# The first batch's transition matrix in units of four target tiles by two source tiles, and its first propagation over four chunks at once in eight PSUM banks

## The chip, the cores and the metric

The kernel runs on one core of one Trainium2 chip. The metric is the device time of one execution in microseconds. Three runs of the kernel before gave 760.93, 761.02 and 761.81 us; their median, 761.02 us, is the time that a forecast is made against. A time below, such as 60.26, is counted in microseconds from the start of the span in the profiled execution.

## The reference, cut to what matters

```python
def _L0_gnn_ref(X, A, Wv, bv, aw, ab, Wk, bk):      # X = relu(layernorm(x)), B = 8, N = 1024, D = 256
    Xw = X @ Wv + bv
    sj, si = Xw @ aw[:d, 0], Xw @ aw[d:, 0]
    e = leaky_relu(sj[:, None, :] + si[:, :, None] + ab[0], negative_slope=0.2)
    alpha_matrix = A * exp(e)
    transition = alpha_matrix / (sum(alpha_matrix, axis=-1, keepdims=True) + 1e-12)
    H, Xk = 0, X
    for k in range(3):
        H = H + Xk @ Wk[k] + bk[k]
        Xk = einsum('bij,bjd->bid', transition, Xk)
    return relu(H)

def _L1_gnn_ref(X, A, kernel, bias):
    Ah = A + eye(N)
    dh = rsqrt(sum(Ah, axis=-1))
    return relu(einsum('bnm,bmf,fc->bnc', dh[:, :, None] * Ah * dh[:, None, :], X, kernel) + bias)

x = x + _L0_gnn_ref(relu(layernorm(x)), adj, ...)
x = x + _L1_gnn_ref(relu(layernorm(x)), adj, ...)
```

## The kernel before, in words

N = 1024 rows are eight tiles of 128. Each fp32 operand of a large product is split into a rounded part (`_hi`, an fp32r copy made by ACT) and a remainder (`_lo`, a subtraction by DVE or POOL), and a product is three matmuls: hi by hi, hi by lo, lo by hi.

`T` is the unnormalised transition matrix, transposed, and is held whole in SBUF as `t_hi` and `t_lo`. It is made in eight units of 1024 columns. In the kernel before, a unit is two target tiles by four source tiles. For each unit ACT forms the leaky scores (`leaky`, line 533, four instructions of 256 columns) and their exponential (`exponent`, 539), DVE multiplies by the adjacency (`t_prod`, 822), ACT rounds (`t_high`, 547), and DVE forms the remainder (`t_low`, 827). Unit `u` needs the adjacency block that the SP or ACT queue has loaded into `tg_a`.

A batch goes through five stages on PE. **U** is the first propagation, eight chunks (one per target tile) of 24 matmuls each. DVE takes each finished chunk out of its bank (`u_chunk`, lines 841, 843, 848, into `tmp`), ACT rounds it (589) and POOL forms its remainder (404). **Dense** is `layer0_dense` of the next batch: for each of its eight tiles six matmuls of 512 columns into `da` and six of 258 into `db`. **V** is the second propagation, **Z** the propagation of layer 1, and the output product follows. In the first batch the units of T are still being made while U runs, so `accumulate_halves` (line 1207) takes chunks 2 to 7 in halves, one half per unit.

The order of all engines is written out by hand: dictionaries name, for each step of a stage, which side work an engine does there (lines 41 to 46, and `rounding` at 584 and `centring` at 911). The side work that matters here, in the first batch's U stage:

- `rows(b, t)` on ACT (564) sums row tile `t` of the adjacency from one of four slots `a_raw`. When it ends, the SP queue loads tile `t + 4` into the slot (276), or, for the last four, the first chunks for Z (290). `diag` (873) on DVE needs the first of those chunks.
- The mean of the next batch is turned by PE into `mean_bank`, a part of `tp` (1084), copied by ACT (`mean_copy`, 452), stored and loaded back as a broadcast by SP (308, 312).
- `centre` (759, DVE) subtracts that mean from the next batch's input, a group of two tiles at a time, `centred_hi` (460, ACT) rounds the group and `centred_lo` (765, DVE) forms its remainder. Dense cannot begin before group 0 is ready.
- Dense of batch 1 also waits until DVE has emptied the banks that U used (`g1_tmp_ready` at 1138), and each tile of `db` waits until DVE has taken the tile before (`dense0`, 780 and 782).

## Time and profile before

| | |
|---|---|
| median of 3 runs (lowest, highest) | 761.02 us (760.93, 761.81) |
| the profiled execution's own time | 761.23 us |
| its span | 759.4 us |
| PE (matmuls), busy in the span | 744.8 us (98%) |
| PE weight load | 684.5 us (90%) |
| DVE | 623.9 us (82%) |
| ACT | 535.4 us (71%) |
| POOL | 188.3 us (25%) |
| mean DMA rate | 189 GB/s |
| U stage of batch 0, first matmul to last matmul's start | 34.27 to 58.20 us |
| dense stage of batch 1, first matmul | 60.26 us |
| V stage of batch 0, first matmul | 79.98 us |

The table is read from the bottom up. PE is busy nearly all the time, so what a change is worth is read from the short stretches in which PE stands still; those in question lie between 34 and 80 us. Busy times are averages over stages that have different limits and don't say which engine the others wait for there. In a row of a timeline, the first number is the start and the second the busy time. Instructions of one engine overlap a little, so the step from one start to the next is about 0.1 us shorter than the busy time on ACT and 0.08 us shorter on DVE.

### The profile page before, as it was taken

How to read it: one execution, taken by the hardware profiler on the slowest of the kernel's cores; microseconds unless marked ns; L12 is line 12 of the kernel's file. 1: busy time of each engine (PE TensorE's matmuls, PEld its weight loads, DVE VectorE, ACT ScalarE, POOL GpSimd, SP SyncE). 2: the span in 40 equal slices, each digit the busy share in tenths (PEclk: the TensorE clock that was granted, in tenths of full speed). 3: DMA queues.
4: the chain of work that ended last, by engine and by line, in shares of the span. 5: the costliest groups of instructions: out<-in, count | busy, mean ns of one | idle time of the engine just before them, and what ended most of it. 6: DMA issues, size and time to landing. Idle time of an engine off the chain costs nothing.

```text
span 759.4 us, 13999 instructions
## 1 busy us (share of the span) xinstructions
PE 744.8 (98%) x5082; PEld 684.5 (90%) x5082; DVE 623.9 (82%) x1415; ACT 535.4 (71%) x1044; POOL 188.3 (25%) x192
## 2 busy tenths in 40 slices
PE   8898999999999999999999999999999999999997
PEld 8696988989899898999979999899988999889986
DVE  6987888878898789887989778897888877986665
ACT  3888795667955789567885679767696667955351
POOL 3041240322403123130322214122150322402230
PEclk9999999999999999999999999999999999999999
DMA  7666448654487255762568625776348654456421
GB/s 234 229 225 205 153 154 285 201 189 152 163 296 235 100 173 193 264 232 87 192 206 274 228 93 171 252 246 210 107 157 281 217 195 144 160 170 195 152 72 56
DMA packets 63909, 143.32 MB, mean 189 GB/s; under 512 B 6768, under 2 KB 32864, under 8 KB 63840
## 3 DMA queue, kind: packets, MB, share of 16 engines
q1 hardware_dynamic: 55072, 111.75, 44.6%
q10 hardware_dynamic: 8768, 30.68, 11.9%
q8 instruction: 40, 0.66, 0.3%
q14 instruction: 29, 0.24, 0.1%
HBM read 133.96 MB, written 8.45 MB: 188 GB/s over the span
## 4 chain that ended last, share of the span: by engine, by line
PE 86%; DVE 6%; ACT 3%; DMA 3%; issue 2%; SPq 0%; DVEq 0%
PE acc L1202 14%; PE acc L1204 14%; PE acc L1203 14%; PE da L1067 14%; PE db L1067 7%; PE da L1168 4%; PE da L1170 4%; PE da L1169 4%; PE tp L1168 4%; PE tp L1170 3%; PE tp L1169 3%; DVE t_raw L822 1%; ACT t_hi L547 1%; DVE t_lo L827 1%; DMA si<-mean_rows_dram 1%
## 5 line engine op out<-in xcount | busy, mean ns | idle before, releaser
L1202 PE MATMUL acc<-g_hi,t_hi 128*128 128x256 f32 (+1 forms) x976 | 276.6, 283 | 0.0
L1204 PE MATMUL acc<-g_hi,t_lo 128*128 128x256 f32 (+1 forms) x976 | 275.2, 282 | 0.0
L1203 PE MATMUL acc<-g_lo,t_hi 128*128 128x256 f32 x976 | 274.6, 281 | 0.0
L1203 PEld LDWEIGHTS acc<-g_lo,t_hi 128*128 128x128 f32 x976 | 184.3, 189 | 0.4
L1202 PEld LDWEIGHTS acc<-g_hi,t_hi 128*128 128x128 f32 x976 | 183.8, 188 | 0.8 <-POOL g_lo L404 0.2
L1204 PEld LDWEIGHTS acc<-g_hi,t_lo 128*128 128x128 f32 x976 | 184.1, 189 | 0.0
L404 POOL TENSOR_TENSOR g_lo<-tmp,g_hi 128x256 fp32r<-128x256 f32 x64 | 61.0, 952 | 263.8 <-ACT g_hi L589 263.8
L833 DVE TENSOR_TENSOR a_lo<-a_raw,a_hi 128x512 fp32r<-128x512 f32 x128 | 94.0, 749 | 23.9 <-ACT a_hi L576 23.9
L533 ACT ACTIVATE tg_e<-si,sij 128x256 f32<-128x256 f32 x256 | 109.1, 499 | 0.1
L576 ACT CAST a_hi<-a_raw 128x512 fp32r<-128x512 f32 x128 | 76.7, 617 | 26.3 <-DVE a_raw L873 17.9
L410 POOL TENSOR_TENSOR hs_lo<-tmp,hs_hi 128x256 fp32r<-128x256 f32 x64 | 60.2, 962 | 89.3 <-ACT hs_hi L473 89.3
L589 ACT CAST g_hi<-tmp 128x256 fp32r<-128x256 f32 x64 | 25.8, 403 | 69.6 <-DVE tmp L848 69.6
L547 ACT CAST t_hi<-t_raw 128x1024 fp32r<-128x1024 f32 x50 | 52.4, 1048 | 27.8 <-DVE t_raw L822 27.8
L399 POOL TENSOR_TENSOR rstd<-ve,mhalf 128x2 f32<-128x2 f32 (+2 forms) x41 | 48.0, 1170 | 95.4 <-DVE ve L731 70.7
L827 DVE TENSOR_TENSOR t_lo<-t_raw,t_hi 128x1024 fp32r<-128x1024 f32 x50 | 68.8, 1376 | 2.2 <-ACT t_hi L547 2.2
L539 ACT ACTIVATE tg_e<-tg_e 128x1024 f32<-128x1024 f32 x64 | 67.8, 1059 | 1.4
L564 ACT ACTIVATE a_raw<-a_raw 128x1024 f32<-128x1024 f32 x64 | 67.6, 1056 | 0.0
L822 DVE TENSOR_TENSOR t_raw<-tg_a,tg_e 128x1024 f32<-128x1024 f32 x50 | 60.9, 1218 | 7.5 <-ACT tg_e L539 7.4
L1168 PE MATMUL tp<-a_hi,hs_hi 128*128 128x512 f32 x128 | 51.4, 401 | 0.0
L469 ACT ACTIVATE tmp<-p,nb,rstd 128x256 f32<-128x256 f32 x64 | 34.9, 593 | 23.2 <-DVE nb L735 22.9
L1168 PE MATMUL da<-a_hi,hs_hi 128*128 128x512 f32 x128 | 51.2, 400 | 0.0
L1169 PE MATMUL tp<-a_lo,hs_hi 128*128 128x512 f32 x128 | 50.5, 395 | 0.0
(169 smaller groups left out, 1604.3 us busy)
## 6 DMA issues: line engine op xcount, KB each, us to landing
a_raw<-adj_dram SPq DMA_DIRECT2D x64, 512.0 KB, 4.3
a_raw<-adj_z_dram SPq DMA_DIRECT2D x64, 512.0 KB, 4.5
tg_a<-adj_t_dram ACTq DMA_DIRECT2D x58, 512.0 KB, 4.2
x_o<-x_dram SPq DMA_DIRECT2D x64, 128.0 KB, 3.4
out_dram<-x_o SPq DMA_DIRECT2D x64, 128.0 KB, 3.9
x_nat<-x_dram SPq DMA_DIRECT2D x28, 256.0 KB, 4.7
xt<-x_t_dram SPq DMA_DIRECT2D x28, 256.0 KB, 4.8
si<-mean_rows_dram SPq DMA_DIRECT2D x7, 512.0 KB, 4.6
```

Source lines behind the costliest of these rows:

```text
L533: ins = nc.scalar.activation(tg_e[:, s, :, q, :], si[:, c].rearrange("p (s i) -> p s i", s=2), ACT.Prelu, bias=sij[:, jt, 0:1], alpha=SLOPE)
L539: nc.scalar.activation(tg_e[:, u % TS], tg_e[:, u % TS], ACT.Exp).then_inc(e_ready, 1)
L576: nc.scalar.copy(a_half(a_hi, i, h), a_raw[:, i % RS, h * N // 2:(h + 1) * N // 2]).then_inc(a_hi_done[h], 1)
L822: nc.vector.tensor_tensor(t_parts(b, u), tg_a[:, s], tg_e[:, s], ALU.mult).then_inc(prod_ready, 1)
L827: nc.vector.tensor_tensor(t_view(t_lo, u), t_parts(b, u), t_view(t_hi, u).bitcast(F32), ALU.subtract).then_inc(t_ready, 1)
L833: nc.vector.tensor_tensor(a_half(a_lo, i, h), a_raw[:, i % RS, h * N // 2:(h + 1) * N // 2], a_half(a_hi, i, h).bitcast(F32), ALU.subtract ...
L1067: ins = nc.tensor.matmul(dst[:, 0:n], l, r, start=(c == 0 and a == 0), stop=(c == len(pairs) - 1 and a == 2))
L1168: nc.tensor.matmul(zt[r][:, f, :], l_hi, r_hi, start=(jt == 0), stop=False)
L1169: nc.tensor.matmul(zt[r][:, f, :], l_hi, r_lo, start=False, stop=False)
L1202: nc.tensor.matmul(acc[:, s, 0:n], l_hi, r_hi, start=(jt == 0), stop=False)
L1203: nc.tensor.matmul(acc[:, s, 0:D], l_hi, r_lo, start=False, stop=False)
L1204: ins = nc.tensor.matmul(acc[:, s, 0:n], l_lo, r_hi, start=False, stop=(jt == NT - 1))
```

## The change

In batch 0 a unit of T is four target tiles by two source tiles, in this order: the first half of the targets by each of four pairs of sources, then the second half. The adjacency of batch 0 is laid out for that on the host. `first_propagation` takes the place of `accumulate_halves`: for each unit it adds the unit's part to four chunks, so that four banks are open at once and eight are used: `acc` (three), `db`, `da` (two) and `tp` (two). The leaky scores of a unit are two instructions of 512 columns. The tables that place the side work change with it.

```diff
-    FIRST_HIGH_U, FIRST_PROD_U, FIRST_LOW_U = {1: 7}, {0: 6, 1: 7}, {0: 5, 1: 6, 2: 7}
+    FIRST_HIGH_U, FIRST_PROD_U, FIRST_LOW_U = {1: 7}, {1: 7}, {1: 6, 2: 7}
-    FIRST_ROWS_U, FIRST_ROWS_D = {2: (0,), 3: (1,), 4: (2,), 6: (3,), 7: (4,)}, {0: (5,), 1: (6,), 3: (7,)}
+    FIRST_ROWS_U, FIRST_ROWS_D = {1: (0,), 2: (1,), 3: (2, 3, 4), 7: (5,)}, {1: (6,), 3: (7,)}
...
-            return [acc[:, s] for s in range(AB)][i % FB] if i % FB < AB else out_bank[i % FB - AB]
+            return (acc[:, 0], acc[:, 1], acc[:, 2], db, da[:, 0], da[:, 1],
+                    tp[:, 0].rearrange("p k c -> p (k c)"), tp[:, 1].rearrange("p k c -> p (k c)"))[i]
...
+        def first_view(t, u):
+
+            iq, jp = u // HJ, u % HJ
+            return t[:, iq * HJ:(iq + 1) * HJ, 2 * jp:2 * jp + 2, :]
...
+            def first_leaky(u):
+
+                iq, jp = u // HJ, u % HJ
+                act.wait_ge(sij0_ready, 2 * jp + 2)
+                act.wait_ge(si_ready, 2 * (iq + 1))
+                for q in range(2):
+                    ins = nc.scalar.activation(slot_view(tg_e, 0, u)[:, :, q, :],
+                                               si[:, iq * HJ * P:(iq + 1) * HJ * P].rearrange("p (s i) -> p s i", s=HJ),
+                                               ACT.Prelu, bias=sij[:, 2 * jp + q, 0:1], alpha=SLOPE)
+                ins.then_inc(leaky_done, 1)
...
-                    rounding = {NT - 3: 0, NT - 1: 1} if b == 0 else {NT - 2: 0, NT - 1: 1}
+                    rounding = {HJ: (0, 1)} if b == 0 else {NT - 2: (0,), NT - 1: (1,)}
...
+                    if b == 0 and i == 0:
+                        leaky(0, NU - 1)
+                        mean_copy(1)
+                        t_high(0, NU - 2, False)
+                        exponent(0, NU - 1)
...
-                if u == NU - 2:
-                    mean_copy(1)
...
-                    if i == (NT - 2 if b == 0 else NT - 1) and not last:
+                    if i == (HJ if b == 0 else NT - 1) and not last:
                         centred_lo(0, b + 1)
+                    if b == 0 and i == 0:
+                        t_low(0, 5)
+                        t_prod(0, 6)
...
-                    centring = {NT - 4: 0, NT - 2: 1} if b == 0 else {NT - 3: 0, NT - 2: 1}
+                    centring = {HJ - 1: (0, 1)} if b == 0 else {NT - 3: (0,), NT - 2: (1,)}
...
-                    pe.wait_ge(g1_tmp_ready, FB)
+                    pe.wait_ge(g1_tmp_ready, HJ + 2)
...
+            def first_propagation():
+
+                for iq in range(2):
+                    for jp in range(HJ):
+                        pe.wait_ge(t_ready, iq * HJ + jp + 1)
+                        for i in range(iq * HJ, (iq + 1) * HJ):
+                            s = first_acc(i)
+                            if iq == 0 and jp == HJ - 1 and i == 2:
+                                rows_of_mean(1)
+                            if i == HJ + 2 and jp == 0:
+
+                                pe.wait_ge(mean_t_ready, 1)
+                            for jt in (2 * jp, 2 * jp + 1):
+                                if i == 0:
+                                    pe.wait_ge(g2_ready, jt + 1)
+                                l_hi, l_lo = t_hi[:, i, jt, :], t_lo[:, i, jt, :]
+                                nc.tensor.matmul(s[:, 0:D + 2], l_hi, g2_hi[:, jt, :], start=(jt == 0), stop=False)
+                                nc.tensor.matmul(s[:, 0:D], l_hi, g2_lo[:, jt, :], start=False, stop=False)
+                                ins = nc.tensor.matmul(s[:, 0:D + 2], l_lo, g2_hi[:, jt, :], start=False, stop=(jt == NT - 1))
+                            if jp == HJ - 1:
+                                ins.then_inc(acc_full, 1)
```

On ACT, at the end of the making of T, this stood before, from the scores of unit 6 on. `bv_r<-tp` is `mean_copy`, and `g_hi<-tmp` is the rounding of a finished chunk:

```order
L533 ACTIVATE tg_e<-si,sij 128x2x128 x4
L452 COPY bv_r<-tp 8x128
L547 CAST t_hi<-t_raw 128x2x512
L539 ACTIVATE tg_e<-tg_e 128x1024
L589 CAST g_hi<-tmp 128x256
L533 ACTIVATE tg_e<-si,sij 128x2x128 x4
L547 CAST t_hi<-t_raw 128x2x512
```

and this stands there now:

```order
L528 ACTIVATE tg_e<-si,sij 128x4x128 x2
L567 CAST t_hi<-t_raw 128x4x256
L559 ACTIVATE tg_e<-tg_e 128x1024
L528 ACTIVATE tg_e<-si,sij 128x4x128 x2
L464 COPY bv_r<-tp 8x128
L567 CAST t_hi<-t_raw 128x4x256
```

The mean's copy moved behind one rounding, one exponential and the scores of the last unit, and the first chunk's rounding moved behind the last exponential.

On ACT, from the rounding of the last unit of T to that of the next batch's input (`ht_hi<-xt`), before:

```order
L547 CAST t_hi<-t_raw 128x2x512
L244 DMA tg_a<-adj_t_dram 128x1024
L589 CAST g_hi<-tmp 128x256
L564 ACTIVATE a_raw,row_a<-a_raw 128x1024
L589 CAST g_hi<-tmp 128x256
L564 ACTIVATE a_raw,row_a<-a_raw 128x1024
L589 CAST g_hi<-tmp 128x256
L564 ACTIVATE a_raw,row_a<-a_raw 128x1024
L460 ACTIVATE ht_hi<-xt 128x512
L589 CAST g_hi<-tmp 128x256 x2
```

and now:

```order
L567 CAST t_hi<-t_raw 128x4x256
L256 DMA tg_a<-adj_t_dram 128x1024
L584 ACTIVATE a_raw,row_a<-a_raw 128x1024
L614 CAST g_hi<-tmp 128x256
L584 ACTIVATE a_raw,row_a<-a_raw 128x1024
L614 CAST g_hi<-tmp 128x256
L584 ACTIVATE a_raw,row_a<-a_raw 128x1024 x3
L472 ACTIVATE ht_hi<-xt 128x512 x2
L614 CAST g_hi<-tmp 128x256 x4
```

Five row sums stand ahead of the input's rounding where three stood.

On DVE, around the remainder of the next batch's group 0 (`ht_lo<-xt`), before:

```order
L848 SCALAR_TENSOR_TENSOR tmp<-da,rinv,p 128x256
L765 SCALAR_TENSOR_TENSOR ht_lo<-xt,ht_hi 128x512
L841 TENSOR_SCALAR row_t<-acc 128x1
L843 RECIPROCAL rinv<-row_t 128x1
L848 SCALAR_TENSOR_TENSOR tmp<-acc,rinv,p 128x256
```

and now:

```order
L848 TENSOR_TENSOR t_lo<-t_raw,t_hi 128x4x256
L862 TENSOR_SCALAR row_t<-db 128x1
L864 RECIPROCAL rinv<-row_t 128x1
L869 SCALAR_TENSOR_TENSOR tmp<-db,rinv,p 128x256
L780 TENSOR_TENSOR xt<-xt,si 128x512 x2
L786 SCALAR_TENSOR_TENSOR ht_lo<-xt,ht_hi 128x512
L862 TENSOR_SCALAR row_t<-da 128x1
L864 RECIPROCAL rinv<-row_t 128x1
L869 SCALAR_TENSOR_TENSOR tmp<-da,rinv,p 128x256
L862 TENSOR_SCALAR row_t<-da 128x1
L864 RECIPROCAL rinv<-row_t 128x1
L869 SCALAR_TENSOR_TENSOR tmp<-da,rinv,p 128x256
```

The remainder moved from after chunk 5 to after chunk 3, and the two chunks in `da` now come behind it.

## Rows read from the trace of the kernel before

**Rows 1.** The page, part 2: the clock granted to PE, in 40 equal slices.

```profile
PEclk9999999999999999999999999999999999999999
```

**Rows 2.** Waits of PE, 34 to 66 us: total, times, longest.

```profile
PE da L1067 <- DVE ht_lo L765: 1.8, 1, 1.8
...
PE db L1067 <- DVE sij L782: 1.4, 1, 1.4
```

**Rows 3.** Timeline of PE: start, busy, line, operation, count, idle time before and releaser.

```profile
34.27 0.28 PE L1202 MATMUL acc<-g_hi,t_hi 128*128 128x258 f32 x1
...
58.20 0.28 PE L1221 MATMUL acc<-g_hi,t_lo 128*128 128x258 f32 x1
...
60.26 0.47 PE L1067 MATMUL da<-wa_hi,ht_hi 128*128 128x512 f32 x1 [1.78 <-DVE ht_lo L765]
...
75.74 0.40 PE L1067 MATMUL da<-wa_hi,ht_hi 128*128 128x512 f32 x1
...
77.14 0.28 PE L1067 MATMUL db<-wb_hi,ht_hi 128*128 128x258 f32 x1
...
77.86 0.40 PE L1067 MATMUL da<-wa_hi,ht_hi 128*128 128x512 f32 x1
...
79.98 0.28 PE L1202 MATMUL acc<-g_hi,t_hi 128*128 128x256 f32 x1
```

**Rows 4.** Timeline of ACT, 25 to 60 us.

```profile
25.07 0.63 ACT L670 CAST wl_hi<-p 128x512 fp32r<-128x512 f32 x1
...
25.59 1.71 ACT L533 ACTIVATE tg_e<-si,sij 128x256 f32<-128x256 f32 x4
...
45.65 1.05 ACT L547 CAST t_hi<-t_raw 128x1024 fp32r<-128x1024 f32 x1 [0.16 <-DVE t_raw L822]
...
52.93 1.05 ACT L547 CAST t_hi<-t_raw 128x1024 fp32r<-128x1024 f32 x1 [1.18 <-DVE t_raw L822]
...
53.89 0.40 ACT L589 CAST g_hi<-tmp 128x256 fp32r<-128x256 f32 x1
...
56.38 1.06 ACT L564 ACTIVATE a_raw<-a_raw 128x1024 f32<-128x1024 f32 x1
...
57.43 0.39 ACT L589 CAST g_hi<-tmp 128x256 fp32r<-128x256 f32 x1
...
58.78 0.61 ACT L460 ACTIVATE ht_hi<-xt 128x512 fp32r<-128x512 f32 x1
```

**Rows 5.** Timeline of DVE, 50 to 69 us.

```profile
50.54 1.23 DVE L827 TENSOR_TENSOR t_lo<-t_raw,t_hi 128x1024 fp32r<-128x1024 f32 x1 [0.66 <-ACT t_hi L547]
...
55.16 0.15 DVE L841 TENSOR_SCALAR row_t<-db 128x1 f32<-128x1 f32 x1
...
55.95 0.15 DVE L841 TENSOR_SCALAR row_t<-da 128x1 f32<-128x1 f32 x1
...
59.42 0.69 DVE L765 SCALAR_TENSOR_TENSOR ht_lo<-xt,ht_hi 128x512 fp32r<-128x512 f32 x1 [0.80 <-ACT ht_hi L460]
...
60.03 0.15 DVE L841 TENSOR_SCALAR row_t<-acc 128x1 f32<-128x1 f32 x1
...
63.55 1.23 DVE L759 TENSOR_TENSOR xt<-xt,si 128x512 f32<-128x512 f32 x1
...
68.61 0.49 DVE L873 TENSOR_TENSOR a_raw<-a_raw,ident 128x128 f32<-128x128 f32 x2 [0.83 <-DMA a_raw<-adj_z_dram]
```

**Rows 6.** Issues of line 276, 50 to 66 us: time from issue to landing.

```profile
DMA to landing us min/median/max: 3.4/4.1/4.3
```

**Rows 7.** Timeline of POOL, 48 to 57 us.

```profile
48.03 1.67 POOL L404 TENSOR_TENSOR g_lo<-tmp,g_hi 128x256 fp32r<-128x256 f32 x1 [2.05 <-ACT g_hi L589]
...
56.55 0.74 POOL L404 TENSOR_TENSOR g_lo<-tmp,g_hi 128x256 fp32r<-128x256 f32 x1 [0.71 <-ACT g_hi L589]
```

**Rows 8.** Timeline of PE at the start of the program.

```profile
1.72 5.38 PE L1099 MATMUL acc<-ident 128*128 128x128 f32 x24 [1.72 <-POOL ident L393]
...
8.40 0.64 PE L1099 MATMUL acc<-ident 128*128 128x128 f32 x4
```

More of the change, by code:

```diff
@@ L237, in t_view, with unit_view, slot_view @@
             return t[:, 2 * cp:2 * cp + 2, jh * HJ:(jh + 1) * HJ, :]
+        def first_view(t, u):
+            iq, jp = u // HJ, u % HJ
+            return t[:, iq * HJ:(iq + 1) * HJ, 2 * jp:2 * jp + 2, :]
+        def unit_view(t, b, u):
+            return first_view(t, u) if b == 0 else t_view(t, u)
+        def slot_view(tg, b, u):
+            part = tg[:, u % TS]
+            return part.rearrange("p s q i -> p (s q i)").rearrange("p (s q i) -> p s q i", s=HJ, q=2) if b == 0 else part
         def a_half(part, i, h):
@@ L247, in t_parts @@
         def t_parts(b, u):
-            return tg_e[:, u % TS] if b > 0 and u < 2 else t_view(t_raw, u)
+            return tg_e[:, u % TS] if b > 0 and u < 2 else unit_view(t_raw, b, u)
         def next_unit(b, u, last):
@@ L517, in leaky @@
                     act.wait_ge(t_ready, b * NU + u - TS + 1)
[L518 to L521 removed]
+                if b == 0:
+                    first_leaky(u)
+                    return
+                if u < 2:
                     act.wait_ge(p0_ready, b * NT + (u + 1) * HJ)
[L524 to L527 removed]
+                if u % HJ == 0:
                     act.wait_ge(si_loaded[u // HJ], 16 * b)
@@ L546, in t_high @@
                 act.wait_ge(prod_ready, b * NU + u + 1)
-                nc.scalar.copy(t_view(t_hi, u), t_parts(b, u)).then_inc(t_hi_done, 1)
+                nc.scalar.copy(unit_view(t_hi, b, u), t_parts(b, u)).then_inc(t_hi_done, 1)
                 nxt = next_unit(b, u, last)
@@ L583, in batch @@
                         mean_copy(b + 1)
-                    rounding = {NT - 3: 0, NT - 1: 1} if b == 0 else {NT - 2: 0, NT - 1: 1}
-                    if i in rounding and not last:
-                        centred_hi(rounding[i], b + 1)
+                    rounding = {HJ: (0, 1)} if b == 0 else {NT - 2: (0,), NT - 1: (1,)}
+                    for g in rounding.get(i, ()) if not last else ():
+                        centred_hi(g, b + 1)
+                    if b == 0 and i == 0:
[3 more added lines that the diff above has]
+                        exponent(0, NU - 1)
                     act.wait_ge(g1_tmp_ready, b * NT + i + 1)
                     nc.scalar.copy(g1_hi[:, i, :], tmp[:, i % 2, :]).then_inc(g1_hi_done, 1)
-                    if i == 0:
+                    if i == 0 and b > 0:
                         leaky(b, NU - 1)
-                        if b == 0:
-                            t_high(0, NU - 2, False)
                         exponent(b, NU - 1)
@@ L910, in batch @@
                             moments0(b + 1)
-                    centring = {NT - 4: 0, NT - 2: 1} if b == 0 else {NT - 3: 0, NT - 2: 1}
-                    if i in centring and not last:
-                        centre(centring[i], b + 1)
+                    centring = {HJ - 1: (0, 1)} if b == 0 else {NT - 3: (0,), NT - 2: (1,)}
+                    for g in centring.get(i, ()) if not last else ():
+                        centre(g, b + 1)
                     if i in OUT_U and b > 0:
@@ L1205, in accumulate @@
                 ins.then_inc(acc_full, 1)
-            def accumulate_halves(cp, middle):
-                for jh in range(2):
-                    pe.wait_ge(t_ready, 2 * cp + jh + 1)
-                    for i in (2 * cp, 2 * cp + 1):
-                        if jh == 1 and i % 2 and middle is not None:
-                            middle()
-                        s = first_acc(i)
-                        if jh == 0 and i >= FB:
-                            pe.wait_ge(g1_tmp_ready, i - FB + 1)
-                        for jt in range(jh * HJ, (jh + 1) * HJ):
-                            l_hi, l_lo = t_hi[:, i, jt, :], t_lo[:, i, jt, :]
-                            nc.tensor.matmul(s[:, 0:D + 2], l_hi, g2_hi[:, jt, :], start=(jt == 0), stop=False)
-                            nc.tensor.matmul(s[:, 0:D], l_hi, g2_lo[:, jt, :], start=False, stop=False)
-                            ins = nc.tensor.matmul(s[:, 0:D + 2], l_lo, g2_hi[:, jt, :], start=False, stop=(jt == NT - 1))
-                        if jh == 1:
-                            ins.then_inc(acc_full, 1)
+            def first_propagation():
[17 more added lines that the diff above has]
+                                ins.then_inc(acc_full, 1)
             def batch(b, last):
@@ L1315 @@
     adj_t = np.ascontiguousarray(adj_t).reshape(B, nt // 2, 2, P, 2, nt // 2 * P)
+    first = adj[0].reshape(2, nt // 2, P, nt // 2, 2, P).transpose(0, 3, 5, 1, 4, 2)
+    adj_t[0] = np.ascontiguousarray(first).reshape(nt // 2, 2, P, 2, nt // 2 * P)
     vecs = np.concatenate([np.asarray(L0_gnn_aw).reshape(-1, P).T, np.asarray(L0_gnn_bv).reshape(-1, P).T,
```

22 lines of the change are left out of this document (6 added, 16 removed).

## The prediction

> **What bounds the kernel now.** I read four views, in this order. The clock row [rows 1] shows that PE is granted full speed in every slice, so a matmul costs the same everywhere. The waits of PE between 34 and 66 us [rows 2] show where it stands still near the change: 1.8 us at the start of the dense stage of batch 1, for the remainder of the input's group 0, and 1.4 us inside that stage, for DVE's take-out of `db`. The timeline of PE [rows 3] gives the frame. The U stage runs from 34.27 to 58.3 us, dense starts at 60.26, and V starts at 79.98. The last of these is the clock to watch. From V on PE is fed without a pause for 30 us, and nothing of the later order changes, so the whole change is worth what it moves 79.98.
>
> The pure matmul work in the frame is fixed. U has 192 matmuls at 0.1187 us, 22.8 us, against 24.0 us taken: a loss of 1.2 us. A tile of dense takes 1.40 + 0.72 = 2.12 us [rows 3], eight take 17.0 us, against 19.72 us from 60.26 to 79.98: a loss of 2.75 us. Between the two stages 1.95 us is lost. With no wait at all V would start at 74.1 us, so at most 5.9 us can be won. The change aims at all three losses. What decides is whether ACT and DVE, which feed the stages, deliver earlier.
>
> **Making T.** Four score instructions of 256 columns become two of 512. One of 256 steps at 0.40 us (1.71 us for four, less the overlap). A plain copy of 512 columns takes 0.63 us [rows 4] and one of 256 takes 0.40, so 256 more columns cost 0.23 and a score instruction of 512 about 0.63 to 0.65. A unit falls from 1.60 to 1.30 us. The bounds are 1.04 (two steps at the plain copy's 0.52) and 1.60 (no gain). The Trainium skill (page "ScalarE: Activation LUTs", section "What ACT_TABLE_LOAD costs") gives 280 ns + 0.833 ns per column with a pointer bias and an overlap of 93 ns. By that, an estimate, a unit would take 1.23 us, and V would come 0.07 us sooner than in my sum.
>
> The gain isn't paid eight times. Before the U stage DVE and PE set the pace, and later the ring of DVE product, ACT rounding and DVE remainder does: each waits for the other, as DVE does for 0.66 us before the remainder of unit 6 [rows 5]. DVE's chunk work for chunks 0 and 1 fills that idle now. So T runs about 0.3 us earlier at unit 5, and 0.25 us earlier at the last rounding: 52.93 [rows 4] becomes 52.7, and ACT is free of it at 53.6.
>
> **The mean's copy.** PE reaches chunk 6 of unit 4 at 34.27 + 4 x 2.85 + 2 x 0.71 = 47.1 us, and now waits there for the mean to leave `tp`. ACT gives the copy only after the rounding of unit 5 (at 45.65 - 0.3 = 45.35 [rows 4], step 0.95), an exponential (0.95) and the last scores (1.30), so at 48.55, and it is out at 48.8. PE loses 1.7 us. The 14 blocks left take 10.0 us and U ends at 58.9, 0.5 us later than before. By itself this costs nothing if dense starts later still, which comes next.
>
> **The start of dense.** From 53.6 us ACT does five row sums and two chunk roundings before the input's rounding, where it did three and three. A row sum steps at 1.05 us (56.38 to 57.43) and a chunk rounding at 0.30 [rows 4]. Four sums and two roundings end at 53.6 + 4.2 + 0.6 = 58.4. The fifth needs tile 4, whose load can be issued only when the first sum is done, at 54.8. Landing took 3.4 to 4.3 us there [rows 6]; I take 4.3, as it competes with two `tg_a` loads and the mean's broadcast, so it lands at 59.1. The fifth sum ends at 60.2. The input's rounding starts then, 1.4 us later than 58.78 [rows 4], and takes 0.61. DVE's remainder follows at 60.85 and steps 0.61 (59.42 to 60.03 [rows 5]). Behind it stand chunks 4 and 5, whose banks dense writes: 0.79 us each (55.16 to 55.95 [rows 5]), with the result in `tmp` 0.87 after the second starts. **Dense starts at 63.15 us, 2.9 us later than before.** PE stands idle from 58.9 to 63.15. The two bounds (landing in 3.4, a unit's scores at 1.04) bring 62.2.
>
> **Inside dense.** The row sums that used to stand between the dense copies on ACT are gone from its first tile, and the first load for Z goes out at 60.2 instead of 64.36, so the 0.83 us wait of DVE for it [rows 5] goes. What stays is the first hand-over of `db`. PE wants it at 63.15 + 1.40 + 0.72 + 1.40 = 66.7. DVE has first to take chunks 6 and 7. Chunk 6 needs its `tmp` slot, which POOL frees one remainder after ACT's rounding of chunk 4, at 62.8 + 0.85 = 63.7. Then come chunk 7, the remainder of group 1 (0.61), centring of group 2 (1.15 [rows 5]) and the take-out of `db` (0.6): 67.3. PE waits 0.7 us once, and I find no further wait: 2.05 of the 2.75 us lost in dense before are won back. POOL's price is the soft one. Its remainder took 1.67 us in one row and 0.74 in another [rows 7]. I take 0.85, since the four from 56 us on took 0.74 to 0.95. With 1.67 throughout, the wait grows by 1.65 and V comes at 82.5.
>
> **The sum.** V starts 2.9 - 2.05 = 0.85 us later, at 80.8. The profiled execution took 761.23 us, 0.2 above the median, so against the median: 761.02 + 0.9 = **761.9 us**. Of the 5.9 us on offer nothing is won, because ACT's side work was moved ahead of the only rounding that PE waits for. A measurement of this kernel tells 0.2%, 1.5 us, from no change, so this counts as no difference. The forecast's own bounds are 760.7 (all low prices: V at 79.7) and 762.4 (scores with no gain, landing 4.5, V at 81.3).
>
> **Rivals.** (1) *Slower, by the clock.* PE would stand still for 4.3 us in one piece, twice as long as anywhere after the start in the kernel before, where the 1.95 us pause left the granted clock at 1.00 [rows 1, 3]. At the start of the program, after PE had done nothing, 24 transposes took 5.38 us, 0.215 apart, while four later ones took 0.64, 0.12 apart [rows 8]. If dense began at that slower step (1.8 times) for the same 5.2 us, it would lose 2.3 us, of which the 0.7 us wait covers a part: V at 82.5, 763.6 us. It decides if the pause is long enough, and a landing in 3.4 us would shorten it to 3.5. The Trainium skill (page "TensorE: Matmul & The Clock Gate", section "Why this matters for your kernels") warns of this: a PE left idle between bursts falls back to half rate and has to earn full rate again. No pause of this length is in the trace, so it neither agrees nor disagrees. Chance 0.20.
>
> (2) *Slower, by POOL's hand-over.* The last four chunks now finish within 2.9 us, and their only way out is `tmp` with two slots, through ACT and POOL. With POOL at 1.67 us V starts at 82.5: 763.5 us. For it: two of the rows around 50 us are that slow. Against: the later ones aren't. It decides above about 1.2 us each. Chance 0.16.
>
> (3) *Faster.* If group 0 were ready by the end of U, as its new place on DVE would allow, dense would start when chunk 5 is out, at 59.7, and V at 77.4: 758.4 us. Against it stand ACT's five sums and two roundings (5.9 us, as above) and the load that can't be issued before 54.8; it would need the sums to run in half their time. Chance 0.06.
>
> **How the numbers follow.** The forecast has 0.58. The range of 760.2 to 764.4 takes in its bounds and both slower rivals with half a microsecond more, and leaves out the faster one and both rivals together. Faster by over 0.2%: 0.06. Within: the forecast's 0.58. Slower: 0.36, the two rivals.
>
> **What would show it.** Right: a wait of PE of about 1.7 us for ACT's copy of the mean near 47 us; the rounding of group 0 at about 60.2, right behind a row sum that waited for a load; PE idle for about 4 us before the first matmul of dense at about 63; one wait for `db` of about 0.7; V at about 80.8. The clock rival shows in a granted clock below 1.00 or in 512-column matmuls further apart than 0.24 us after the pause. The POOL rival shows in DVE waiting for POOL before chunks 6 and 7. I am wrong in the mechanism if group 0's rounding comes before 58.8 or dense starts before 61.

## The result and the profile after

| | before | after |
|---|---|---|
| median of 7 runs each (lowest, highest) | 761.03 us (760.56, 762.75) | 764.26 us (763.97, 767.27) |
| ratio, 95% interval | | 1.0046 (1.0031 to 1.0061) |
| profiled execution, its span | 761.23, 759.4 | 764.22, 762.4 |
| U of batch 0, first matmul | 34.27 | 34.14 |
| idle time of PE ahead of dense, from its row | 1.78 | 4.58 |
| dense of batch 1, first matmul | 60.26 | 63.51 |
| V of batch 0, first matmul | 79.98 | 82.15 |

The idle time is the one that PE's own row gives, from the end of the last matmul; the 1.95 us of the prediction counts the same pause from the last matmul's start plus one step. Idle times of PE below are all of the first kind.

The changed kernel is slower by 3.2 us, more than the 0.2% that a measurement of it can tell. The forecast was no difference. 764.26 lies just inside the range, among the slower rivals.

The waits of PE between 34 and 82 us after the change (compare [rows 2]):

```profile
PE da L1091 <- DVE tmp L869: 4.6, 1, 4.6
PE tp L1247 <- ACT bv_r L464: 1.2, 1, 1.2
```

The pause at dense has grown from 1.8 to 4.6 us, and a wait for the mean's copy (`bv_r`) is new. Both were forecast. The waits for `db` of the kernel before, 1.8 us in two pieces by 82 us, are gone. Who is late is seen on ACT in the timeline of the same execution (compare [rows 4]; idle time and its releaser in brackets):

```profile
56.64 1.05 ACT L584 ACTIVATE a_raw<-a_raw 128x1024 f32<-128x1024 f32 x1
...
59.49 1.06 ACT L584 ACTIVATE a_raw<-a_raw 128x1024 f32<-128x1024 f32 x1 [0.67 <-DMA a_raw<-adj_dram]
...
60.55 1.13 ACT L472 ACTIVATE ht_hi<-xt 128x512 fp32r<-128x512 f32 x2
```

The row sums follow each other from 56.64 on, the last of them has waited 0.67 us for its load, and the rounding of the input (`ht_hi`) starts at 60.55, where it started at 58.78. DVE stands still for it, and chunks 4 and 5 stand behind it:

```profile
56.01 1.35 DVE L780 TENSOR_TENSOR xt<-xt,si 128x512 f32<-128x512 f32 x2
61.19 0.69 DVE L786 SCALAR_TENSOR_TENSOR ht_lo<-xt,ht_hi 128x512 fp32r<-128x512 f32 x1 [3.84 <-ACT ht_hi L472]
...
62.19 0.48 DVE L869 SCALAR_TENSOR_TENSOR tmp<-da,rinv,p 128x256 f32<-128x256 f32 x1
...
62.97 0.48 DVE L869 SCALAR_TENSOR_TENSOR tmp<-da,rinv,p 128x256 f32<-128x256 f32 x1
```

DVE idles 3.84 us, gives `ht_lo` at 61.19, and then chunk 5's `tmp` at 62.97, which releases dense. The granted clock of the stretch (stretch, length, busy times and counts of PE, PEld, DVE, ACT and POOL, clock, DMA share, GB/s):

```profile
63.00:64.00 1.00, 0.49 (x1) 0.50 (x2) 0.68 (x3) 0.51 (x2) 0.76 (x2) 0.68 0.97 389
...
65.00:66.00 1.00, 1.00 (x4) 0.81 (x3) 1.00 (x2) 0.68 (x2) 0.93 (x2) 0.50 0.00 0
66.00:67.00 1.00, 1.00 (x7) 0.90 (x6) 1.00 (x2) 1.00 (x3) 0.90 (x1) 0.62 0.00 0
67.00:68.00 1.00, 1.00 (x7) 0.86 (x7) 0.97 (x4) 1.00 (x3) 0.00 (x0) 1.00 0.33 45
```

Before, it was at full speed throughout [rows 1]. Now it is 0.50, the lower of the two levels (1.2 of 2.4 GHz), from 64 to 66 us and partly so on either side. The slow matmuls are seen one by one:

```profile
64.10 0.63 PE L1091 MATMUL da<-wa_lo,ht_hi 128*128 128x512 f32 x1
64.52 0.63 PE L1091 MATMUL da<-wa_hi,ht_lo 128*128 128x512 f32 x1
...
66.23 0.42 PE L1091 MATMUL db<-wb_hi,ht_hi 128*128 128x258 f32 x1
66.44 0.42 PE L1091 MATMUL db<-wb_lo,ht_hi 128*128 128x258 f32 x1
...
67.20 0.40 PE L1091 MATMUL da<-wa_hi,ht_hi 128*128 128x512 f32 x1
```

512 columns start 0.43 us apart where 0.24 is usual, 258 columns 0.21 apart. The tile takes 3.69 us (63.51 to 67.20) against 2.12 before the change [rows 3], 1.57 us more.

### The profile page after: what moved, and what is told of

Read it like the earlier page. It is cut to its first block, busy times and chain, and to the rows that moved or that the text cites. A ratio compares the mean times of both kernels' runs of the same rounds, so it can differ in the third digit from the quotient of the medians.

```text
span 762.4 us, 13989 instructions
## 1 busy us (share of the span) xinstructions
PE 744.8 (98%) x5082; PEld 684.9 (90%) x5082; DVE 623.4 (82%) x1415; ACT 533.4 (70%) x1028; POOL 187.8 (25%) x192
## 4 chain that ended last, share of the span: by engine, by line
PE 87%; DVE 6%; DMA 3%; ACT 2%; issue 2%; SPq 0%; DVEq 0%
PE da L1091 14%; PE acc L1226 14%; PE acc L1228 14%; PE acc L1227 14%; PE db L1091 7%; PE da L1192 4%; PE da L1194 4%; PE da L1193 4%; PE tp L1192 3%; PE tp L1194 3%; PE tp L1193 3%; DVE t_raw L843 1%; DVE t_lo L848 1%; DMA x_nat<-x_dram 1%; ACT t_hi L567 1%
## 5 line engine op out<-in xcount | busy, mean ns | idle before, releaser
L1226 PE MATMUL acc<-g_hi,t_hi 128*128 128x256 f32 (+1 forms) x960 | 272.0, 283 | 0.0
L1228 PE MATMUL acc<-g_hi,t_lo 128*128 128x256 f32 (+1 forms) x960 | 270.6, 282 | 0.0
L1227 PE MATMUL acc<-g_lo,t_hi 128*128 128x256 f32 x960 | 270.1, 281 | 0.0
L1227 PEld LDWEIGHTS acc<-g_lo,t_hi 128*128 128x128 f32 x960 | 181.2, 189 | 0.3
L1226 PEld LDWEIGHTS acc<-g_hi,t_hi 128*128 128x128 f32 x960 | 180.7, 188 | 0.8 <-POOL g_lo L416 0.2
L1228 PEld LDWEIGHTS acc<-g_hi,t_lo 128*128 128x128 f32 x960 | 181.1, 189 | 0.0
L416 POOL TENSOR_TENSOR g_lo<-tmp,g_hi 128x256 fp32r<-128x256 f32 x64 | 60.2, 942 | 266.9 <-ACT g_hi L614 266.8
L553 ACT ACTIVATE tg_e<-si,sij 128x256 f32<-128x256 f32 x224 | 95.5, 499 | 0.2 <-DMA si<-si_rows_dram 0.2
L422 POOL TENSOR_TENSOR hs_lo<-tmp,hs_hi 128x256 fp32r<-128x256 f32 x64 | 60.1, 960 | 88.8 <-ACT hs_hi L485 88.8
L1091 PE MATMUL da<-wa_hi,ht_hi 128*128 128x512 f32 x112 | 45.4, 405 | 5.4 <-DVE tmp L869 4.6
```

Source lines behind the costliest of these rows:

```text
L553: ins = nc.scalar.activation(tg_e[:, s, :, q, :], si[:, c].rearrange("p (s i) -> p s i", s=2), ACT.Prelu, bias=sij[:, jt, 0:1], alpha=SLOPE)
L1091: ins = nc.tensor.matmul(dst[:, 0:n], l, r, start=(c == 0 and a == 0), stop=(c == len(pairs) - 1 and a == 2))
L1226: nc.tensor.matmul(acc[:, s, 0:n], l_hi, r_hi, start=(jt == 0), stop=False)
L1227: nc.tensor.matmul(acc[:, s, 0:D], l_hi, r_lo, start=False, stop=False)
L1228: ins = nc.tensor.matmul(acc[:, s, 0:n], l_lo, r_hi, start=False, stop=(jt == NT - 1))
```

## Experiments

The starts of U drift by some tenths of a microsecond from one execution to the next, so V is counted from U's first matmul. That is 45.71 us in the kernel before, and 48.01 in the changed one. Eleven runs were measured in three groups, each on another chip and each beside the kernel before: the four from "pause filled" to "before, sums ahead" on one, the next four ("low parts behind", "all three", "changed again", "filled again") on a second, the last three on a third. The median of before was 761.13, 761.34 and 761.59 us in them. The last column is the ratio to it with its interval. The times of dense and V come from one execution of each run, and that one isn't always typical: with the pause filled, the copy early and the sums behind it was the fastest of its run, with the low parts behind and the pause filled again the slowest.

| kernel | dense | V | V after U's start | median | ratio |
|---|---|---|---|---|---|
| before | 60.26 | 79.98 | 45.71 | | |
| changed | 63.51 | 82.15 | 48.01 | 764.26 | 1.0046 (1.0031, 1.0061) |
| pause filled | 63.52 | 81.67 | 47.63 | 764.26 | 1.0037 (1.0023, 1.0050) |
| copy early | 62.73 | 81.44 | 47.53 | 763.59 | 1.0033 (1.0022, 1.0044) |
| sums behind | 60.04 | 79.59 | 45.53 | 761.49 | 1.0004 (0.9995, 1.0014) |
| before, sums ahead | 62.38 | 81.01 | 46.92 | 762.24 | 1.0013 (1.0004, 1.0022) |
| low parts behind | 63.20 | 82.75 | 48.50 | 763.10 | 1.0017 (1.0008, 1.0026) |
| all three | 60.31 | 78.93 | 44.72 | 760.44 | 0.9992 (0.9982, 1.0001) |
| changed again | 64.71 | 84.02 | 49.66 | 765.69 | 1.0055 (1.0043, 1.0067) |
| filled again | 67.36 | 85.54 | 48.60 | 765.42 | 1.0048 (1.0034, 1.0061) |
| fifth sum behind | 61.76 | 80.42 | 46.36 | 761.67 | 1.0003 (0.9994, 1.0012) |
| sums, low behind | 60.67 | 79.64 | 45.31 | 761.00 | 0.9990 (0.9981, 0.9999) |
| all three again | 60.26 | 78.43 | 44.11 | 760.50 | 0.9991 (0.9980, 1.0002) |

**Is it the row sums?** In the changed kernel they go back behind the roundings of chunks 4, 5 and 6:

```diff
-    FIRST_ROWS_U, FIRST_ROWS_D = {1: (0,), 2: (1,), 3: (2, 3, 4), 7: (5,)}, {1: (6,), 3: (7,)}
+    FIRST_ROWS_U, FIRST_ROWS_D = {1: (0,), 2: (1,), 4: (2,), 5: (3,), 6: (4,), 7: (5,)}, {1: (6,), 3: (7,)}
```

> The changed kernel with the row sums 2, 3 and 4 moved behind the rounding of the next batch's input (U steps 4, 5 and 6 in place of all three at step 3). Theory: the rounding of group 0 comes at about 56.5 instead of 60.55, dense starts at 59.4 to 60.0, PE's pause before it is under 1.5 us and the clock stays at the upper level; the waits inside dense are between 1.5 and 2.5 us, V starts at 78.3 to 79.2, and the time is 759.3 to 760.3, faster than before the change. Rival (the four-chunk order with its late take-out through two slots is the brake): dense can't start before 62 and V not before 81.

Measured: 761.49 us, that of before, and V 45.53 us after U's start. The waits of PE, 34 to 82 us:

```profile
PE tp L1247 <- ACT bv_r L464: 1.2, 1, 1.2
PE da L1091 <- DVE tmp L869: 1.2, 1, 1.2
PE db L1091 <- DVE sij L803: 0.9, 1, 0.9
PE da L1091 <- DVE g_lo L820: 0.4, 1, 0.4
```

The pause is 1.2 us, the wait for the copy stands as it was, and the clock keeps full speed. So the order of the sums carries the loss, 2.48 us of V, and the rival is refuted. The gain that I had expected didn't come: V at 79.59 is later than 79.2, and the time isn't below that of before. The new units with these sums behind gain 0.18 us of V and nothing in the median. (In the kernel before the third sum stands ahead of the rounding; here it stands behind.)

**Do the sums cost as much without the rest of the change?** The kernel before gets the sums' new places:

```diff
-    FIRST_ROWS_U, FIRST_ROWS_D = {2: (0,), 3: (1,), 4: (2,), 6: (3,), 7: (4,)}, {0: (5,), 1: (6,), 3: (7,)}
+    FIRST_ROWS_U, FIRST_ROWS_D = {2: (0,), 3: (1,), 4: (2, 3, 4), 7: (5,)}, {1: (6,), 3: (7,)}
```

> The kernel before with only the side-work table moved: row sums 2, 3 and 4 at U step 4, ahead of the rounding of group 0, the later ones as in the change. Units, chunks and banks are those of before. Theory (the place of the sums does the harm, whatever the units): group 0 is rounded at 60.8 instead of 58.78, dense starts at about 62.2 after a pause of 3.7 us, V starts at 80.5 to 81.5 (80.5 if the clock stays up, 81.5 if it falls after this pause), and the time is 761.7 to 763. Rival (units and banks do the harm): within 0.5 us of before.

Measured: V 46.92 us after U's start, 1.21 more than before, 762.24 us, as expected. Dense starts 2.30 us later, counted from U, after a pause of 4.11 us, and the granted clock falls to 0.50 here too; V loses only half of that, since the 1.8 us of waits for `db` in the kernel before are gone. Alone the sums cost half of what they cost in the changed kernel. By these traces the two parts together cost 1.27 us more than the sum of each alone (2.30 against 1.21 - 0.18). That is an estimate from one trace each: a second trace of the changed kernel (below) has V 1.65 us later than the first.

**Is it one sum, and its load?** Only the fifth sum goes behind the rounding of the input, the third and fourth stay ahead:

```diff
-    FIRST_ROWS_U, ... = {1: (0,), 2: (1,), 3: (2, 3, 4), 7: (5,)}, ...
+    FIRST_ROWS_U, ... = {1: (0,), 2: (1,), 3: (2, 3), 4: (4,), 7: (5,)}, ...
```

> The changed kernel with one edit: the fifth row sum of batch 1 (the one that waits for its load) stands behind the rounding of chunk 4, and so behind the two high parts of ht, not ahead of them. Nothing is left out. Theory A (the fifth sum costs its 1.05 us and the wait for its load, 0.67 to 1.70 us in the four changed kernels traced so far in which it waits long): the two high parts start at 58.6 to 59.3 instead of 60.55 to 61.75, dense 0 starts at 61.5 to 62.2, V starts 46.2 to 46.9 us after the first propagation (48.01 and 49.66 in the two traces of the changed kernel), and the medians lose the most of all one-edit runs: 1.5 to 2.5 us below the changed kernel. Theory B (only the work of the sum counts, since the load is awaited anyway by what follows): V starts 46.9 to 47.2 us after the first propagation.

Measured: 761.67 us, V 46.36 after U's start. V is where theory A had it; the time is 2.6 us under the changed kernel's, a little more than its 1.5 to 2.5. ACT, 57 to 62 us:

```profile
57.76 1.04 ACT L584 ACTIVATE a_raw<-a_raw 128x1024 f32<-128x1024 f32 x1
...
58.80 1.13 ACT L472 ACTIVATE ht_hi<-xt 128x512 fp32r<-128x512 f32 x2
...
61.26 1.05 ACT L584 ACTIVATE a_raw<-a_raw 128x1024 f32<-128x1024 f32 x1
```

The rounding starts at 58.80, 1.75 us earlier, dense 1.75 earlier, and V 1.65. The sum behind it finds its load there. Of the 2.48 us of V of the three sums one alone carries 1.65. The median says more: with this one sum moved it is that of before already (1.0003), as it is with all three moved (1.0004), so the medians leave nothing measurable for the other two. The time of this sum splits into 1.05 of work and 0.67 of waiting for the load, as ACT's rows showed. The second part varies: the wait was 0.67, 0.77, 1.28, 1.38 and 1.70 us in five executions in which it stood out. The three long ones are all of the second group of runs, on one chip. The chip doesn't settle it, though: the same load took from issue to landing 4.5, 3.8 and 5.7 us in three runs of the first group (pause filled, copy early, sums behind), and 3.8 to 5.4 in the second. The same kernel, traced again, shows how far this reaches:

> The changed kernel once more, not edited, beside the run with the filled pause on the same chip. Theory A (V's start carries 2.3 us, the wait at 157 for ht_lo behind a late x_nat load is chance and comes and goes with the landing time): median 763.2 to 764.3, V 48.0 us after the first propagation as before within 0.2, the wait at 157 between 0 and 1.0. Theory B (the wait at 157 belongs to the change: everything behind V runs 2.2 us later against the loads): it is there again with 0.8 to 0.9 us.

```profile
58.28 1.05 ACT L584 ACTIVATE a_raw<-a_raw 128x1024 f32<-128x1024 f32 x1
...
60.70 1.06 ACT L584 ACTIVATE a_raw<-a_raw 128x1024 f32<-128x1024 f32 x1 [1.28 <-DMA a_raw<-adj_dram]
...
61.75 1.13 ACT L472 ACTIVATE ht_hi<-xt 128x512 fp32r<-128x512 f32 x2
```

The load came 1.2 us later than in the first trace (60.70 against 59.49), the rounding with it, and dense at 64.71. Half of the 1.2 us is this load's time from issue to landing, 5.0 us against 4.4, and half its later issue (55.70 against 55.12 us): U had begun 0.2 us later, and DVE had waited 0.28 us for an adjacency block at 44 us. V came 49.66 us after U's start, outside what I expected (within 0.2 of 48.0), and the median of 765.69 too. Nothing in the kernel was altered; the part of the loss that hangs on transfers isn't a constant. The wait at 157 us didn't recur (below).

**Why do the sums cost more in the new order?** There the take-out of chunks 4 and 5 stands behind `ht_lo` on DVE. The low parts go behind chunk 5:

```diff
-                    if i == (HJ if b == 0 else NT - 1) and not last:
+                    if i == (HJ + 2 if b == 0 else NT - 1) and not last:
                         centred_lo(0, b + 1)
```

> The changed kernel with one edit: the low parts of ht of the next batch's first half are taken behind chunk 5's combination on VectorE, not ahead of chunk 4's. Nothing is left out. Theory A (what the change gave away over the row sums' price in the old order, 2.3 us of V's start against 1.2, is that chunks 4 and 5, whose banks dense 0 writes, stand behind the wait for ht_hi on VectorE): 1.6 us of VectorE's work moves into its 3.84 us of idle time, dense 0 starts at 61.7 to 62.1 instead of 63.51, TensorE's pause is 2.8 to 3.2 us instead of 4.6, and V starts 46.6 to 47.2 us after the first propagation (48.01 in the changed kernel); median 1.0 to 1.5 us below the changed kernel's. Theory B (only the slow ScalarE chain decides, the order on VectorE is covered): dense 0 starts earlier, but V not more than 0.3 us earlier, the time is the changed kernel's within 0.5 us.

Measured: dense at 63.20 and V at 48.50, both outside what was expected when held against the first trace. But the fifth sum waited 1.38 us for its load here:

```profile
60.66 1.06 ACT L584 ACTIVATE a_raw<-a_raw 128x1024 f32<-128x1024 f32 x1 [1.38 <-DMA a_raw<-adj_dram]
...
61.72 1.13 ACT L472 ACTIVATE ht_hi<-xt 128x512 fp32r<-128x512 f32 x2
```

The fair partner is the changed kernel of the same group, whose rounding started at the same time (61.75). Against it dense comes 1.51 us sooner and V, from U's start, 1.16; the two traced executions differ by 1.5 us (765.38 and 763.88), and the medians by 2.6, more than V explains; the execution traced here was the slowest of eleven. Both gains in V and in dense are of the size that theory A gave. The 1.16 us would be most of the 1.27 us of the interaction; with one trace of each that is likely, not shown. With the sums out of the way too (two edits), does the order on DVE still count?

> The changed kernel with two edits: the row sums behind the roundings of chunks 4, 5 and 6, and the low parts of ht behind chunk 5's combination; the mean's copy stays where the change put it. Nothing is left out. Theory A (the order on VectorE still costs something without the sums, because chunk 5's combination released dense 0 in that run, 1.20 us after the first propagation): dense 0 starts at 59.6 to 60.1, V starts 44.6 to 45.2 us after the first propagation (45.53 with the sums alone behind, 44.72 with all three), the time 0 to 0.8 us below the kernel before. Theory B (the copy is what the three edits won on the run with two): V 45.3 to 45.6 after the first propagation, the time that of the kernel before within 0.4.

Measured: V 45.31 us after U's start, 0.22 less than with the sums alone behind, in theory B's span, and dense at 60.67, later than theory A's 60.1. The median of 761.00 is 0.6 under before, so theory A's time came with theory B's trace; the traced execution took 761.70, near the top of its run. Two traces of one kernel differ by more than 0.22 us, so this leaves open whether the order still counts.

**What does the clock cost?** 36 matmuls of 258 columns, whose result nobody reads, fill the pause:

```diff
                     first_propagation()
+                    pe.wait_ge(g1_tmp_ready, 3)
+                    for _ in range(36):
+                        nc.tensor.matmul(acc[:, 2, 0:D + 2], t_hi[:, 7, 7, :], g2_hi[:, 7, :], start=True, stop=True)
```

> The changed kernel with 36 matmuls of 258 columns (4.3 us, nobody reads their result) right behind its U stage, where PE stood idle for 4.59 us. Nothing else changes. Theory (the pause lets the clock fall, and its 3.3 us at the lower level cost PE 1.35 us in dense): dense still starts at 63.5, its 512-column matmuls are 0.24 us apart from the first on, one wait of about 0.7 us for the db bank appears, V starts at 80.8 to 81.1 instead of 82.15, and the time falls by about 1.2 us to 763.0. Rival (dense is late through the hand-overs between DVE, ACT and POOL, and the slow matmuls only fill time in which PE would have waited): V stays at 82.0 to 82.2 and the time at 764.2.

The stretches and then the waits of PE with the pause filled:

```profile
62.00:64.00 2.00, 1.63 (x12) 1.38 (x11) 1.58 (x7) 0.81 (x2) 0.75 (x2) 1.00 0.86 340
64.00:66.00 2.00, 2.00 (x14) 1.74 (x13) 1.89 (x5) 1.06 (x3) 1.64 (x3) 1.00 0.45 184
66.00:68.00 2.00, 1.30 (x6) 0.72 (x4) 2.00 (x5) 2.00 (x5) 0.92 (x1) 1.00 0.03 8
```

```profile
PE db L1091 <- DVE sij L803: 0.8, 1, 0.8
```

The clock stays at 1.00, dense starts at the same time (63.52), and V comes at 81.67, 0.48 us sooner, later than the theory had it and sooner than the rival. The slow tile had lost 1.57 us, but with full speed PE now waits 0.75 for `db`: DVE sets the pace of this stretch, and slow matmuls hide behind it. The median is the same, 764.26, as the rival had it. Because the question was close, both kernels ran once more side by side:

> The changed kernel with 36 matmuls of 258 columns (their sum is never read) in TensorE's pause ahead of dense 0, once more, beside the changed kernel on the same chip. Theory A (the fall to a granted clock of 0.50 in dense 0 costs at most what V's start showed, 0.4 us, because VectorE sets dense 0's pace): granted clock 1.00 throughout, V 47.5 to 47.8 us after the first propagation, median 0.2 to 0.5 us below the changed kernel's of this call. Theory B (the clock's fall costs what rival 1 of the prediction said, 1.7 us): median 1.4 to 2.0 us below it.

From dense to V the changed kernel took 19.31 us and the filled one 18.18, a price of 1.13. In the changed kernel the clock was at 0.50 for longer this time, after the longer pause (5.2 us):

```profile
63.00:64.00 1.00, 0.00 (x0) 0.00 (x0) 0.90 (x6) 0.09 (x1) 0.00 (x0) 0.50 1.07 373
...
68.00:69.00 1.00, 1.00 (x6) 1.00 (x5) 0.63 (x1) 1.00 (x3) 0.09 (x1) 0.50 0.00 0
```

The medians differ by 0.27 us (765.69 and 765.42). So the fall costs 0.5 to 1.1 us of V in the traces and too little to see in the medians. Theory A's median came out in the second pair and theory B's did not, but the V that A gave did not either: 48.60 after U's start, where 47.5 to 47.8 was expected, since the fifth sum waited 1.70 us for its load. (In that execution all is late from before U on, which began at 36.94: the granted clock was 0.50 from 11 to 16 us.)

The first trace of the changed kernel shows the mildest case. Its mean granted clock was 0.998, the highest of the seven executions; the other six had 0.993 to 0.996. With the pause filled the five had 0.999 to 1.000. In the second pair it was 0.990 to 0.996 against 0.995 to 1.000. So filling gave back most of the clock, not only in the traced executions, and the medians hardly moved. An estimate: 0.995 over 762 us is 7.6 us at the lower clock, if all of it stands here, as in the second trace of the changed kernel (0.995), where the price was 1.13.

**The mean's copy** goes back to its place before:

```diff
                         leaky(0, NU - 1)
-                        mean_copy(1)
...
                 leaky(0, u)
+                if u == NU - 2:
+                    mean_copy(1)
```

> The changed kernel with the mean's copy where it stood before, right behind the scores of unit 6. Theory (ACT's chain of sums and roundings sets the start of dense, and the 1.2 us wait at 47.4 is hidden by it): the wait at 47 us goes, U ends 0.9 to 1.3 us earlier at about 57.8, dense starts at 63.3 to 63.6 all the same, the pause grows to about 5.7 us, and the time is 764.2 within 0.5, or up to 1 us more if the longer pause keeps the clock down longer. Rival (the wait for the mean is what makes the change slower): V comes 1.2 us earlier and the time falls to 763.0.

```profile
PE da L1092 <- DVE tmp L870: 4.4, 1, 4.4
PE da L1248 <- DVE t_lo L849: 0.8, 1, 0.8
```

The wait of 1.2 us becomes one of 0.8 for the last unit's remainder. U ends 0.62 us sooner, dense starts 0.78 sooner and V 0.48 sooner (from U's start), 763.59 us. Theory and rival both missed: dense moved, and V by far less than 1.2 us. The trace doesn't put this down to U's earlier end. Counted from U's start, the load for the fifth sum was issued at the same time as without the edit (20.97 and 20.98 us); it landed in 3.8 us instead of 4.4, and the rounding behind it came 0.55 us sooner. The mean's broadcast, another load, was issued 1.0 us earlier here (48.75 against 49.78). Whether that made room or the landing was chance isn't shown, and the intervals of the two ratios overlap. So it stays open whether the copy costs anything.

**All three together:** sums behind, copy early, low parts behind.

> The changed kernel with three edits at once: the row sums where they delay nothing (sums 2, 3 and 4 behind the roundings of chunks 4, 5 and 6), the copy of the next batch's mean ahead of the last unit as in the kernel before, and the low parts of ht behind chunk 5's combination. Nothing is left out. Theory A (three separate costs: 2.5 us of V's start for the row sums, about 0.5 for the copy, 1.3 or more for the order on VectorE of which the row sums' place hides a part): dense 0 starts at 59.1 to 59.5, right behind the first propagation, and V starts 43.9 to 44.7 us after the first propagation (45.7 before), the time 1.0 to 1.8 us below the kernel before. Theory B (the batches behind pay it back, since the x_nat loads and the mean's chain of batches 1 and 2 have no slack): V starts as early, but the second propagation of batch 1 waits, and the time is within 0.7 us of the kernel before.

> The changed kernel with all three edits once more, not edited further, to see whether it beats the kernel before by more than the measurement can tell. Theory A (V starts 1.0 us earlier than before, and the batches behind keep it): V 44.5 to 44.9 us after the first propagation, median 0.7 to 1.3 us below the kernel before. Theory B (the batches behind pay it back where a load lands late): V as early, the median within 0.6 us of the kernel before.

V came 44.72 and 44.11 us after U's start, 1.0 and 1.6 less than before. The medians are 760.44 and 760.50, 0.90 and 1.09 us below before, with intervals that just reach 1.0 (0.9982 to 1.0001 and 0.9980 to 1.0002). Both groups point the same way, at 0.13%; it is under what a measurement of this kernel tells by itself, and I claim no more. Both times the gain is more than theory B's 0.7 and 0.6. Of theory A's times the first (1.0 to 1.8) is just missed and the second (0.7 to 1.3) met; V is at its late edge first (44.7) and earlier than its 44.5 then. The waits that are left in the second of the two traces, 34 to 82 us:

```profile
PE da L1092 <- DVE ht_lo L787: 1.5, 1, 1.5
PE da L1248 <- DVE t_lo L849: 0.8, 1, 0.8
PE da L1092 <- DVE g_lo L821: 0.2, 1, 0.2
```

Dense again waits for `ht_lo`, 1.5 us. Its rounding started at 57.01 and 56.96 in the two traces, behind a product of DVE for the last unit that took 1.75 and 1.76 us where 1.22 is usual.

## Why the prediction was wrong

**Making T: the gain was lost again.** Two score instructions took 1.32 us and stepped by 1.22, better than the 1.30 of the forecast. But the last rounding of T started at 52.99, where 52.7 was forecast (52.93 before): ACT had waited 1.77 us for DVE's product of that unit, which took 1.77 us where the forecast had the usual 1.23 (row of 51.19 us at the end).

```profile
52.99 1.05 ACT L567 CAST t_hi<-t_raw 128x1024 fp32r<-128x1024 f32 x1 [1.77 <-DVE t_raw L843]
```

**The mean's copy: right in place, smaller.** PE waited 1.20 us instead of 1.7, from 47.36, and U ended at 58.92 (forecast 58.9). "By itself this costs nothing" is neither shown nor refuted: moving it back won 0.48 us of V, all of it with a load that landed sooner.

**The start of dense: right, and late by what T was late.** The rounding came at 60.55 (60.2), behind a fifth sum that waited for its load; `ht_lo` at 61.19 (60.85); dense at 63.51 (63.15). The landing was sized well. SP issued the load at 55.12 where 54.8 was forecast, and it took 4.4 us where 4.3 was taken (the rows of SP's issues from there, and of the first alone with its time to landing):

```profile
55.12 4.42 SPq L288 DMA_DIRECT2D a_raw<-adj_dram  x4
```

```profile
a_raw<-adj_dram SPq DMA_DIRECT2D x1, 512.0 KB, 4.4
```

So of the 0.36 us some 0.3 come from the slow product in the making of T, and 0.1 from the landing.

**Inside dense: the step that failed.** The prediction put 17.65 us between dense and V (63.15 to 80.8) and measured 18.64. With the clock held at full speed it was 18.15. So 0.5 us was dense's own pace, and 0.5 the clock's fall. Of the first, 0.3 lies at the hand-over of `db`: PE idled 0.75 us for it, as forecast at 0.7, but the tile with it took 3.14 us (65.73 to 68.87) against 2.12: 1.02 lost where the forecast had 0.7. The first tile and one at 75.22 took 0.1 us more each, and the others 2.11 to 2.13. The sum of V is then closed: 80.8 + 0.36 + 0.50 + 0.49 = 82.15. Three small terms, all on the same side, make 1.35 us. For dense's pace a sum over matmuls without waits, a lower bound, had been taken for a value. The fall of the clock had been left out of the sum and put into a rival.

**Rival 1** gave 0.20 to a clock that falls after the pause, with V at 82.5 and 763.6 us. The clock did fall, and V was at 82.15. So the rival named the event, and its chance was too low: a pause more than twice the longest that the trace showed at full speed should have been held likelier to cost the clock than not. Yet its price was wrong as well. It let the slow stretch run 5.2 us and cost 1.7 of V; it ran 3.3 and cost 0.5, since DVE's work, not PE's, paced the stretch. So that V came near 82.5 and the time near 763.6 is in part luck: the rival's cause carries 0.5 of the 2.2 us. (In the second pair the slow stretch in dense ran 4.7 us and cost 1.1.) Its step of 1.8 times was right, 0.43 against 0.24 us, though the rows it was taken from don't show a fall: the granted clock reads 1.00 there, in the first 12 us of the kernel before. The Trainium skill (page "TensorE: Matmul & The Clock Gate", section "Why this matters for your kernels") warns that TensorE drops back to half rate when it stands idle between bursts of matmuls. This trace agrees in kind: full speed in the kernel before with 1.78 us of idle time, 0.50 after 4.58.

**Rival 2**, POOL's hand-over at 1.67 us each, did not come: two remainders behind each other took 1.52 us, and two more 1.88.

**From V to the time: the second step that failed.** The prediction let every microsecond of V count once, and nothing behind it. V was 2.17 us later, the span 3.0 longer. The rest is 0.16 us up to U of batch 1, 0.56 of a wait further on, in dense of the next batch, and 0.1 behind that. The row of before, then that of after:

```profile
154.88 0.47 PE L1067 MATMUL da<-wa_hi,ht_hi 128*128 128x512 f32 x1 [0.29 <-DVE ht_lo L765]
```

```profile
157.76 0.47 PE L1091 MATMUL da<-wa_hi,ht_hi 128*128 128x512 f32 x1 [0.85 <-DVE ht_lo L786]
```

It waits for `ht_lo`, behind the mean and the last of the `x_nat` loads, which took 6.01 us to land against 4.60 before. PE waits there in both kernels. In the second trace of the changed kernel no wait over 0.3 us stood there, but the filled one had 0.52 us of it at 160.7 us and the first trace with all three edits 0.60 at 429. It comes and goes from one execution to the next, so I don't count it to the change. Whether the transfers' later place makes it likelier wasn't tried and stays open.

**The chances.** 0.58 for no difference stood on a bound of 762.4 for the forecast itself, only 0.15 below the line of 0.2%. With V's own error of a few tenths and a wait that hangs on a landing time, the cases above the line should have had the larger share.

## What to carry to other kernels

Ask of each instruction that is moved ahead of a hand-over not only what it takes, but whether its data will be there: one row sum of 1.05 us, moved ahead of a rounding, put off the start of V, two stages on, by 1.65 us, since it waited for a load that could be issued only when an earlier sum had freed its slot. Order an engine's queue so that what another engine stands still for comes first, and whatever awaits a transfer behind it. And an end that is built from matmul time without waits is a floor: where several terms all can only add, take the middle above their sum.
